# A vision tower on one NeuronCore: the table stage's third power and doublings, one load's queue, and the order of the last group's end

## The chip, the cores and the metric

The kernel runs on one core of one Trainium2 chip. The core has five instruction streams that meet only at semaphores: TensorE (PE in the profile; its weight loads are PEld) for matrix products, VectorE (DVE) and ScalarE (ACT) for elementwise work, GpSimd (POOL), and SyncE (SP), which here only issues transfers. ScalarE issues transfers too. SBUF is the on-chip memory, PSUM the eight banks that TensorE writes. The metric is the device time of one execution, in microseconds (us), lower is better. A profiled execution has a span, from its first to its last instruction, and a time of its own that is a little longer.

## What is computed

The reference builds a state-space convolution kernel from H = 256 channels and N = 64 complex states, and then runs an attention block and a soft decision tree on its result:

```python
dA = (1 + dtA / 2) / (1 - dtA / 2)
V = exp(log(dA)[:, :, None] * arange(256))          # powers 0..255 of one number per (h, n)
h = 2 * einsum('chn,hnl->chl', C * B, V).real       # tokens, (16, 256, 256)
h = h + attention_block(layernorm(h))                # linear attention, gelu MLP
h = h + tree_ffn(layernorm(h))                       # 255 routers, 256 leaves
```

The powers of the number w = dA are products of three short tables: w to the 0..7 (`Er`, `Ei`), B times w to the 0, 8, ..., 56 (`X`, `Y`), and U to the 1..3, where U is w to the 64.

## The kernel before

Each engine's program is written out by hand, and that text is the only thing that sets the order. An engine waits in order: what stands behind a waiting instruction waits with it.

**Table stage.** SyncE loads `log_dt`, both halves of `inv_A_real` (`iar`) and B, ScalarE's queue loads `A_imag` (`aim`). VectorE and ScalarE compute w and square it seven times, in steps of one instruction each (L1009, L1011; ScalarE's squares L627, L630); `base[9]` and `base[10]` hold the squared moduli in turn. On one tile that is 128 partitions (64 states, real and imaginary convention) by 256 channels. Then VectorE forms U's third power (real part in `U[:, 0, 2, :]`, imaginary in `ui[:, 2, :]`) with six operations out of U and its square. Last come three doublings of X and Y: from m entries to 2m, m = 1, 2, 4. The entries of a channel lie together, 8 of X and then 8 of Y, so for m = 1 an operation on X touches one number in every 16. GpSimd meanwhile makes `Er` and `Ei` (L461 to L466).

**Token stage.** Sixteen chunks of 16 channels. For chunk n ScalarE copies the X, Y rows to PSUM (`paired_tables`, L678, which needs the finished X and Y), VectorE makes the products and their sum M (`products`, L1044, `product_sums`, L1052), GpSimd makes the weights Wa and Wb (`rotate`, L494), and TensorE multiplies them (`tokens`, L1480, 64 products). Buffers are double: M of chunk n and the weights of chunk n wait for the tokens of n - 2. ScalarE evicts (`token_out`, L692), and its order for each chunk is: tables of chunk n + 2, token eviction of chunk n, store, Wa's copy and M's copy of chunk n + 2.

**Combined weights.** Before its first token product TensorE multiplies small weight matrices (L1540, L1545) and forms the MLP's bias (L1550, one column each). It begins when the seventh weight, `fc2raw`, has landed. Then `pe_set` is 3; ScalarE copies the bias (L754, `b1copied`), and only after `b1copied` does TensorE go on to chunk 0.

**Middle.** Norms, q, k, v, linear attention, the MLP and the tree run in a software pipeline over groups of four tiles. The change touches none of it.

**The end.** The last group is done in two halves h = 0, 1 of two tiles. For a half: x4 is transposed into one PSUM bank, split into a high and a low part (`last_x4_high` on ScalarE, `last_x4_low` on VectorE), multiplied by the gates (`last_gate`), a tanh, eight levels of the tree on VectorE (`last_tree`), leaf probabilities transposed (`last_lT`) and split (`last_leaf_high`, `last_leaf_low`, L933, L1427), multiplied by the leaves (`last_leaf`), and added to `o1` (`last_finish`, L1434). GpSimd makes `o1` of each half (`last_out_bias`, L597), but only after VectorE's `finish(LAST - 1)` (L1275), which reads the old `o1`. SyncE stores the four tiles (L442).

Of the kernel before, what the change touches and what calls it, by code (L numbers as in the profile page):

```python
# [5 lines left out]
ALU = mybir.AluOpType  # L6
# [4 lines left out]
P = 128  # L11
# [16 lines left out]
LOGS = 8  # L28
# [23 lines left out]
DVE_U = DVE_POWERS + 6 * 4  # L52
# [10 lines left out]
def vit_tower(nc, logdt, inv_ar, a_im, b_ri, c_ri, n1g, n1b, qkvT, projT, proj_b, n2g, n2b, fc1T, fc1_b,  # L63
              fc2T, fc2_b, wq, routersT, leafT, woutT, wout_b, consts, out):
    with ExitStack() as ctx:
# [177 lines left out]
        ld_bias = sem("ld_bias")  # L243
# [37 lines left out]
        def last_out(h):  # L281
            return PS[:, 2 + h, :].rearrange("p (t d) -> p t d", t=2)

# [37 lines left out]
        def _(sp):  # L321
            halves = [slice(r * N, (r + 1) * N) for r in range(2)]
            sp.dma_start(ldt[:, :], logdt.unsqueeze(0).to_broadcast([P, H])).then_inc(ld_exp, 16)
            for rows in halves:
                sp.dma_start(iar[rows, :], inv_ar).then_inc(ld_exp, 16)
# [118 lines left out]
            sp.wait_ge(outst, CREDIT + 32 * LAST + 64)  # L444
# [162 lines left out]
        def _(act):  # L607
            for r in range(2):
                act.dma_start(aim[r * N:(r + 1) * N, :], a_im).then_inc(ld_aim, 16)
# [15 lines left out]
            for j in range(1, LOGS - 1):  # L625
# [4 lines left out]
                act.activation(PS[:, 0, 0:H], power(j)[0], ACT.Square).then_inc(act_tab, 1)  # L630

# [7 lines left out]
            for d in range(ND - 1):  # L639
                if d == 2:  # L640
                    act.wait_ge(dve_set, DVE_POWERS + 6)
                act.activation(U[:, 1, d, :], ui[:, d, :], ACT.Copy, scale=sgn[:, 0:1]).then_inc(u_out, 1)
# [274 lines left out]
            def last_x4_high(h):  # L917
                act.wait_ge(zxT[h], CREDIT + 1)
                act.wait_ge(gtmm, CREDIT + LAST)
                act.activation(last_x(x4Th, h), last_out(h), ACT.Copy).then_inc(zxh[h], 1)  # L920
# [41 lines left out]
            last_leaf_high(1)  # L962


        @block.vector
        def _(dve):
# [47 lines left out]
            t = PS[:, 2, 0:H]  # L1014
            for to, op, first, second in ((U[:, 0, 2, :], ALU.subtract, 0, 1), (ui[:, 2, :], ALU.add, 1, 0)):
                (ar, ai), (br, bi) = power(6), power(7)
                tt(t, ai, (br, bi)[second], ALU.mult)
                tt(to, ar, (br, bi)[first], ALU.mult)
                tt(to, to, t, op)
            dve.wait_ge(b_out, 2)  # L1020
            for j, m in ((0, 1), (1, 2), (2, 4)):
                dve.wait_ge(pw_out, j + 1)
                wr, wi = (PS[:, (6, 7, 1)[j], x * H:(x + 1) * H].unsqueeze(2).to_broadcast([P, H, m])
                          for x in range(2))
                t = PS[:, 2:4, :].rearrange("p b x -> p (b x)")[:, 0:H * m].rearrange("p (h m) -> p h m", m=m)
# [372 lines left out]
            def last_x4_low(h):  # L1398
                dve.wait_ge(zxh[h], CREDIT + 1)
                dve.wait_ge(gtmm, CREDIT + LAST)  # L1400
                dve.tensor_tensor(last_x(x4Tl, h), last_out(h), last_x(x4Th, h).bitcast(F32),
                                  ALU.subtract).then_inc(zxl[h], 1)
# [21 lines left out]
            def last_leaf_low(h):  # L1424
                dve.wait_ge(zlh[h], CREDIT + 1)
                dve.wait_ge(lvmm, CREDIT + LAST)
                dve.tensor_tensor(last_x(lTl, h), last_out(h), last_x(lTh, h).bitcast(F32),  # L1427
                                  ALU.subtract).then_inc(zll[h], 1)
# [31 lines left out]
            last_tree(1, 0, LEVELS)  # L1460
            last_leaf_low(0)
            finish(LAST - 1)
# [6 lines left out]
        def _(pe):  # L1469
# [67 lines left out]
            pe.wait_ge(dve_set, DVE_POWERS)  # L1537
# [342 lines left out]
```

## Time and profile before

| | |
|---|---|
| time, median of 3 runs | 508.58 us (508.49 to 510.35) |
| time of the profiled execution | 508.74 us |
| its span | 507.0 us |
| mean granted TensorE clock | 0.986 |
| busy: PE, DVE, ACT, POOL | 86%, 71%, 57%, 39% of the span |
| TensorE before its first product at 32.06 us | idle |
| chain that ended last, over the whole span | PE 69%, DVE 17%, issue 5%, ACT 4%, POOL 2% |
| landing of fc2raw after its issue | 10.6 us |

The busy shares are means over three unlike stages. In the middle TensorE never stops; in the first 73 us and in the last 15 us it waits, and there the chain of waits names other engines. A time in the views is counted from the start of the span.

### The profile page before, as it was taken

To read this page: it belongs to the slowest core of one execution; us is meant where nothing else is said; L and a number is where in the kernel's file an instruction comes from. 1 tells how busy PE (TensorE), PEld (TensorE's weight loads), DVE (VectorE), ACT (ScalarE), POOL (GpSimd) and SP (SyncE) were. 2 spreads that over 40 slices of the span, in tenths; PEclk is the share of its full clock that TensorE was granted. 3 is DMA by queue.
4 is the path that set the end of the run, shared out by engine and by line. 5 is a ranking of instruction groups with operands and counts; after the bars stand their busy time and mean duration, and the time that the engine had idled before them with its cause. 6 is when DMAs were issued, how large, how long until landed. Compare 5 with 4: busy or idle time off the path is not lost.

```text
span 507.0 us, 11410 instructions
## 1 busy us (share of the span) xinstructions
PE 434.1 (86%) x3808; PEld 398.1 (79%) x3808; DVE 357.8 (71%) x870; ACT 291.1 (57%) x604; POOL 195.5 (39%) x185
## 2 busy tenths in 40 slices
PE   0047663999899999999999999999999999998974
PEld 0037653888788898888988988988988988998973
DVE  5899998995877685547476476476476576485684
ACT  3805553788876777566457457457447448446630
POOL 0497998761241210515406306306307207206001
PEclk9998997999999999999999999999999999999998
DMA  4532665344343101101002002002002001001002
GB/s 125 184 127 75 166 170 172 95 137 138 112 121 100 63 22 43 41 1 43 1 1 83 0 0 83 0 0 83 0 0 83 0 0 41 0 0 43 3 0 84
DMA packets 39903, 30.95 MB, mean 61 GB/s; under 512 B 19520, under 2 KB 35264, under 8 KB 39872
## 3 DMA queue, kind: packets, MB, share of 16 engines
q1 hardware_dynamic: 29312, 27.81, 17.9%
q10 hardware_dynamic: 10560, 2.75, 2.3%
q8 instruction: 16, 0.26, 0.2%
q14 instruction: 15, 0.12, 0.1%
HBM read 17.97 MB, written 12.58 MB: 60 GB/s over the span
## 4 chain that ended last, share of the span: by engine, by line
PE 69%; DVE 17%; issue 5%; ACT 4%; POOL 2%; DMA 1%; DVEq 1%; SPq 0%; POOLq 0%; ACTq 0%
PE PS L315 18%; PE PS L317 18%; PE PS L316 18%; PE PS L1488 5%; PE PS L1598 3%; PE PS L1530 3%; PE PS L1480 3%; DVE M L1052 2%; DVE Mb L1044 2%; DVE XY L976 2%; DVE lTl L1215 1%; DVE PS L976 1%; PE PS L1497 1%; DVE outb L1275 1%; DVE PS L1044 1%
## 5 line engine op out<-in xcount | busy, mean ns | idle before, releaser
L1244 DVE TENSOR_TENSOR gl<-PS,gh 128x512 fp32r<-128x512 f32 x56 | 38.7, 690 | 62.2 <-ACT gh L811 34.4
L808 ACT ACTIVATE PS<-PS,fc1bias 128x512 f32<-128x512 f32 x56 | 36.7, 656 | 75.2 <-PE PS L317 74.3
L315 PE MATMUL PS<-fc2h,gh 128*128 128x256 f32 x256 | 73.7, 288 | 2.9 <-DVE gl L1244 1.5
L542 POOL TENSOR_SCALAR pst<-mv 128x4 f32<-128x4 f32 x15 | 4.2, 282 | 185.3 <-DVE pst L1228 185.3
L317 PE MATMUL PS<-fc2l,gh 128*128 128x256 f32 x256 | 71.5, 279 | 0.0
L316 PE MATMUL PS<-fc2h,gl 128*128 128x256 f32 x256 | 71.4, 279 | 0.0
L315 PE MATMUL PS<-x2Th,fc1h 128*128 (+2 forms) x144 | 54.4, 378 | 0.0
L315 PEld LDWEIGHTS PS<-fc2h,gh 128*128 128x128 f32 x256 | 48.0, 188 | 7.0 <-DVE pst L1228 1.6
L316 PE MATMUL PS<-x2Th,fc1l 128*128 (+2 forms) x144 | 53.0, 368 | 0.0
L317 PE MATMUL PS<-x2Tl,fc1h 128*128 (+2 forms) x144 | 52.9, 367 | 0.0
L1480 PE MATMUL PS<-M,Wa 128*64 128x64 f32 x512 | 35.1, 237 | 16.7 <-DVE M L1052 14.8
L316 PEld LDWEIGHTS PS<-fc2h,gl 128*128 128x128 f32 x256 | 48.2, 188 | 1.0
L317 PEld LDWEIGHTS PS<-fc2l,gh 128*128 128x128 f32 x256 | 48.0, 188 | 0.0
L1480 PEld LDWEIGHTS PS<-M,Wa 128*64 128x64 f32 x512 | 32.2, 146 | 19.6 <-DVE M L1052 12.8
L811 ACT ACTIVATE gh<-PS 128x512 fp32r<-128x512 f32 x56 | 33.6, 599 | 2.8
L1480 PE MATMUL PS<-M,Wb 128*64 128x64 f32 x512 | 34.3, 233 | 0.0
L1480 PEld LDWEIGHTS PS<-M,Wb 128*64 128x64 f32 x512 | 32.2, 149 | 0.0
L1540 PE MATMUL PS<-routraw,wqraw 128*128 128x256 f32 x8 | 3.8, 654 | 32.1 <-DMA fc2raw<-in_fc2T 32.1
L317 PEld LDWEIGHTS PS<-x2Tl,fc1h 128*128 128x128 f32 x144 | 27.1, 188 | 4.7
L494 POOL TENSOR_TENSOR Wa<-craw,U 128x768 f32<-128x768 f32 x16 | 25.7, 1607 | 9.9 <-PE PS L1480 7.7
L315 PEld LDWEIGHTS PS<-x2Th,fc1h 128*128 128x128 f32 x144 | 27.1, 189 | 2.5
L316 PEld LDWEIGHTS PS<-x2Th,fc1l 128*128 128x128 f32 x144 | 27.2, 189 | 2.3
(233 smaller groups left out, 1402.7 us busy)
## 6 DMA issues: line engine op xcount, KB each, us to landing
h<-h_scratch SPq DMA_DIRECT2D x16, 256.0 KB, 3.7
q_scratch<-qe SPq DMA_DIRECT2D x16, 256.0 KB, 2.2
qf<-q_scratch SPq DMA_DIRECT2D x16, 256.0 KB, 2.9
out_tokens<-outb SPq DMA_DIRECT2D x14, 256.0 KB, 2.3
h_scratch<-tokev ACTq DMA_DIRECT2D x10, 256.0 KB, 3.0
craw<-in_c_ri SPq DMA_DIRECT2D x16, 128.0 KB, 2.6
craw<-in_c_ri SPq DMA_DIRECT2D x32, 64.0 KB, 2.4
h_scratch<-tokev SPq DMA_DIRECT2D x6, 256.0 KB, 2.8
```

Source lines behind the costliest of these rows:

```text
L315: pe.matmul(dst, ah, bh, start=start, stop=False, **kw)
L316: pe.matmul(dst, al, bh, start=False, stop=False, **kw)
L317: return pe.matmul(dst, ah, bl, start=False, stop=stop, **kw)
L494: pool.tensor_tensor(w[:, par, :, :, 1:ND].rearrange("p h c d -> p d h c"), c, u, ALU.mult).then_inc(wdone, 1)
L808: act.activation(bank(j % 2), bank(j % 2), ACT.Gelu, bias=fc1bias[:, j:j + 1]).then_inc(gact, 1)
L811: act.activation(gh[:, j % 2, :], bank(j % 2), ACT.Copy).then_inc(gact, 1)
L976: link(dve.tensor_tensor(out_, a, b, op))
L1044: dve.tensor_tensor(to, x, w, ALU.mult).then_inc(vdone, 1)
L1244: dve.tensor_tensor(gl[:, j % 2, :], bank(j % 2), gh[:, j % 2, :].bitcast(F32), ALU.subtract).then_inc(gldone, 1)
L1480: mm = pe.matmul(dst, w[:, par, i, :, :].rearrange("p c d -> p (c d)"), M[:, par, i, :, :].rearrange("p a e -> p (a e)"), start=x == 0, st ...
L1488: mm = pe.transpose(PS[:, b + k, t * P:(t + 1) * P], src[:, t, k * P:(k + 1) * P], ident)
L1530: mm = pe.matmul(PS[:, sums_bank(c), k * (P + 1):(k + 1) * (P + 1)], key, value, start=half == 0 and k == 0, stop=half == 1, skip_group_ch ...
```

## The change

- **Third power.** With s = 4 times the square of U's real part, the third power's imaginary part is (s - modulus squared) times U's imaginary part, and its real part is (s - 3 times modulus squared) times U's real part. The square of the real part was already in PSUM, and ScalarE makes the threefold modulus with one more operation.
- **Doublings.** X and Y are multiplied by the real part in one operation over both. For m = 1 and 2 the sum is one operation as well.
- **Load.** The second half of `iar` is issued first on ScalarE's queue instead of third on SyncE's.
- **End.** For half 1 each transposed column block has a PSUM bank of its own (`last_turned`), and the copies, low parts and products go block by block; `last_rows_out` now runs over the block outside and the tile inside, for both halves. VectorE takes `last_leaf_low(0)` after level 4 of the second tree instead of after its last level. The odd tiles are stored from ScalarE's queue.
- TensorE's wait for the tables before its weight products names a count two higher.

```diff
             sp.dma_start(ldt[:, :], ...).then_inc(ld_exp, 16)
-            for rows in halves:
-                sp.dma_start(iar[rows, :], inv_ar).then_inc(ld_exp, 16)
+            sp.dma_start(iar[halves[0], :], inv_ar).then_inc(ld_exp, 16)
...
             for half in range(HALVES):
-                for c in range(2):
-                    sp.wait_ge(zout[half], CREDIT + c + 1)
-                    sp.dma_start(out[2 * LAST + c, half * P:(half + 1) * P, :],
-                                 x2[:, 2 * half + c, :]).then_inc(outst, 16)
+                sp.wait_ge(zout[half], CREDIT + 1)
+                sp.dma_start(out[2 * LAST, ...], x2[:, 2 * half, :]).then_inc(outst, 16)
...
         def _(act):
+            act.dma_start(iar[N:P, :], inv_ar).then_inc(ld_exp, 16)
             for r in range(2):
                 act.dma_start(aim[r * N:(r + 1) * N, :], a_im).then_inc(ld_aim, 16)
...
+            act.wait_ge(act_tab, 5 + 2 * (LOGS - 2))
+            act.activation(base[:, 9, :], base[:, 10, :], ACT.Copy, scale=3.0).then_inc(act_tab, 1)
...
             def last_leaf_high(h):
-                act.wait_ge(zlT[h], CREDIT + 1)
                 act.wait_ge(lvmm, CREDIT + LAST)
-                act.activation(last_x(lTh, h), last_out(h), ACT.Copy).then_inc(zlh[h], 1)
+                if h == 0:
+                    act.wait_ge(zlT[h], CREDIT + 1)
+                    act.activation(last_x(lTh, h), last_out(h), ACT.Copy).then_inc(zlh[h], 1)
+                else:
+                    for k in range(KD):
+                        act.wait_ge(zlT[h], CREDIT + k + 1)
+                        act.activation(lTh[:, k, HT:2 * HT], last_turned(h, k), ACT.Copy).then_inc(zlh[h], 1)
+            def last_store(half):
+                act.wait_ge(zout[half], CREDIT + 2)
+                act.dma_start(out[2 * LAST + 1, ...], x2[:, 2 * half + 1, :]).then_inc(lastst, 16)
...
-            for to, op, first, second in ((U[:, 0, 2, :], ALU.subtract, 0, 1), (ui[:, 2, :], ALU.add, 1, 0)):
-                (ar, ai), (br, bi) = power(6), power(7)
-                tt(t, ai, (br, bi)[second], ALU.mult)
-                tt(to, ar, (br, bi)[first], ALU.mult)
-                tt(to, to, t, op)
+            link(dve.scalar_tensor_tensor(PS[:, 3, 0:H], ur2, 4.0, base[:, 10, :], ALU.mult, ALU.subtract))
+            dve.wait_ge(act_tab, 7 + 2 * (LOGS - 2))
+            link(dve.scalar_tensor_tensor(PS[:, 2, 0:H], ur2, 4.0, base[:, 9, :], ALU.mult, ALU.subtract))
+            tt(ui[:, 2, :], PS[:, 3, 0:H], ui1, ALU.mult)
+            tt(U[:, 0, 2, :], PS[:, 2, 0:H], ur, ALU.mult)
...
-                tt(t, y, wi, ALU.mult)
-                tt(x_, x, wr, ALU.mult)
-                tt(x_, x_, t, ALU.add)
-                tt(t, x, wi, ALU.mult)
-                tt(y_, y, wr, ALU.mult)
-                tt(y_, y_, t, ALU.subtract)
+                if m < 4:
+                    tt(t, xy, wr, ALU.mult)
+                    tt(x_, y, wi, ALU.mult)
+                    link(dve.scalar_tensor_tensor(y_, x, -1.0, wi, ALU.mult, ALU.mult))
+                    tt(xy_, xy_, t, ALU.add)
+                else:
+                    tt(xy_, xy, wr, ALU.mult)
+                    tt(t, y, wi, ALU.mult)
+                    tt(x_, x_, t, ALU.add)
+                    tt(t, x, wi, ALU.mult)
+                    tt(y_, y_, t, ALU.subtract)
...
-            last_tree(1, 0, LEVELS)
+            last_tree(1, 0, 5)
             last_leaf_low(0)
+            last_tree(1, 5, LEVELS)
             finish(LAST - 1)
             last_leaf_low(1)
...
-            pe.wait_ge(dve_set, DVE_POWERS)
+            pe.wait_ge(dve_set, DVE_POWERS + 2)
...
-                for t in range(2):
-                    x = slice(h * HT + t * P, h * HT + (t + 1) * P)
-                    for k in range(KD):
+                for k in range(KD):
+                    if h == 1 or k == 0:
+                        pe.wait_ge(high, CREDIT + k + 1)
+                        pe.wait_ge(low, CREDIT + k + 1)
+                    for t in range(2):
+                        x = slice(h * HT + t * P, h * HT + (t + 1) * P)
                         mm = three(pe, last_rows(h, t), ah[:, k, x], al[:, k, x], wh[:, k, :], wl[:, k, :],
                                    k == 0, k == KD - 1)
-                    mm.then_inc(done, 1)
+                        if k == KD - 1:
+                            mm.then_inc(done, 1)
```

Below is VectorE's program in the table stage before, from the first operation of the third power through the first half of the m = 1 doubling (its last two rows come once more for Y). PS is PSUM, XY holds X and Y, U and ui the powers of U.

```order
L976 TENSOR_TENSOR PS<-ui 128x256
L976 TENSOR_TENSOR U<-U 128x256
L976 TENSOR_TENSOR U<-U,PS 128x256
L976 TENSOR_TENSOR PS<-ui,U 128x256
L976 TENSOR_TENSOR ui<-U,ui 128x256
L976 TENSOR_TENSOR ui<-ui,PS 128x256
L976 TENSOR_TENSOR PS<-XY,PS 128x256
L976 TENSOR_TENSOR XY<-XY,PS 128x256 x2
```

And the same place in the changed kernel, through the whole m = 1 doubling:

```order
L1035 SCALAR_TENSOR_TENSOR PS<-PS,base 128x256
L1037 SCALAR_TENSOR_TENSOR PS<-PS,base 128x256
L996 TENSOR_TENSOR ui<-PS,ui 128x256
L996 TENSOR_TENSOR U<-PS,U 128x256
L996 TENSOR_TENSOR PS<-XY,PS 128x512
L996 TENSOR_TENSOR XY<-XY,PS 128x256
L1053 SCALAR_TENSOR_TENSOR XY<-XY,PS 128x256
L996 TENSOR_TENSOR XY<-XY,PS 128x512
```

Six operations have become four, each with an operand in PSUM, and the six of a doubling have become four, two of them twice as wide.

The second place is VectorE's end, before: th, lpA and lpB are the tree's tiles, lTl the low part of the leaf probabilities, outb the tile of the group before the last, x the last group's result.

```order
L1418 SCALAR_TENSOR_TENSOR lpA<-th,lpB 128x2x16
L1421 SCALAR_TENSOR_TENSOR lpA<-lpB,lpA 128x2x16
L1418 SCALAR_TENSOR_TENSOR lpB<-th,lpA 128x2x32
L1421 SCALAR_TENSOR_TENSOR lpB<-lpA,lpB 128x2x32
L1418 SCALAR_TENSOR_TENSOR lpA<-th,lpB 128x128
L1421 SCALAR_TENSOR_TENSOR lpA<-lpB,lpA 128x128
L1418 SCALAR_TENSOR_TENSOR lpB<-th,lpA 128x256
L1421 SCALAR_TENSOR_TENSOR lpB<-lpA,lpB 128x256
L1427 TENSOR_TENSOR lTl<-PS,lTh 128x2x256
L1275 TENSOR_TENSOR outb<-PS,o_132 128x512 x2
L1427 TENSOR_TENSOR lTl<-PS,lTh 128x2x256
L1434 TENSOR_TENSOR x_123<-PS,o_132 128x256 x4
```

And in the changed kernel:

```order
L1456 SCALAR_TENSOR_TENSOR lpA<-lpB,lpA 128x2x16
L1463 TENSOR_TENSOR lTl<-PS,lTh 128x2x256
L1453 SCALAR_TENSOR_TENSOR lpB<-th,lpA 128x2x32
L1456 SCALAR_TENSOR_TENSOR lpB<-lpA,lpB 128x2x32
L1453 SCALAR_TENSOR_TENSOR lpA<-th,lpB 128x128
L1456 SCALAR_TENSOR_TENSOR lpA<-lpB,lpA 128x128
L1453 SCALAR_TENSOR_TENSOR lpB<-th,lpA 128x256
L1456 SCALAR_TENSOR_TENSOR lpB<-lpA,lpB 128x256
L1304 TENSOR_TENSOR outb<-PS,o_132 128x512 x2
L1468 TENSOR_TENSOR lTl<-PS,lTh 128x256 x2
L1475 TENSOR_TENSOR x_123<-PS,o_132 128x256 x4
```

The low part of half 0 has moved ahead of the last six tree operations; that of half 1 is two narrow operations, still behind `finish`.

## Rows read from the trace of the kernel before

**Rows 1.** Chain of waits, 0 to 80 us: start, us, what.
```profile
1.80 3.41 DMA iar<-in_inv_ar
...
19.20 0.45 DVE PS L976
...
23.10 0.62 DVE PS L976
...
38.86 0.40 ACT PS L678
...
73.17 2.15 PE PS L1480 x64
```
**Rows 2.** Timeline, SyncE's queue at the start: start, us, engine, line, operation.
```profile
1.19 1.19 SPq L325 DMA_DIRECT2D iar<-in_inv_ar  x2
```
**Rows 3.** Groups by form, 19 to 39 us: count, busy us, mean ns, idle before.
```profile
L976 DVE TENSOR_TENSOR XY<-XY,PS 128x1024 f32<-128x1024 f32 x4 | 4.9, 1220 | 0.1
...
L976 DVE TENSOR_TENSOR XY<-XY,PS 128x512 f32<-128x512 f32 x4 | 2.8, 688 | 0.1
L976 DVE TENSOR_TENSOR XY<-XY,PS 128x256 f32<-128x256 f32 x4 | 2.5, 614 | 0.1
...
L976 DVE TENSOR_TENSOR ui<-U,ui 128x256 f32<-128x256 f32 x1 | 1.2, 1153 | 0.0
...
L1011 DVE SCALAR_TENSOR_TENSOR U<-PS,base 128x256 f32<-128x256 f32 x1 | 0.4, 425 | 0.1
```
**Rows 4.** Timelines by engine, 32 to 50 us, in order of time.
```profile
32.06 3.78 PE L1540 MATMUL PS<-routraw,wqraw 128*128 128x256 f32 x8 [32.06 <-DMA fc2raw<-in_fc2T]
...
37.46 3.63 PE L1550 MATMUL PS<-nrm,fc1raw 128*128 128x1 f32 x32
...
41.13 0.18 ACT L754 ACTIVATE b1add<-PS 128x8 f32<-128x8 f32 x1
...
42.78 0.49 PE L1480 MATMUL PS<-M,Wa 128*64 128x64 f32 x4 [1.69 <-DVE M L1052]
...
46.40 0.60 ACT L692 ACTIVATE tokev<-PS 128x512 f32<-128x512 f32 x1 [3.84 <-PE PS L1480]
...
46.74 1.64 POOL L494 TENSOR_TENSOR Wa<-craw,U 128x768 f32<-128x768 f32 x1 [2.92 <-PE PS L1480]
...
48.54 0.47 ACT L678 ACTIVATE PS<-XY 128x256 f32 x1
...
49.62 1.10 DVE L1044 TENSOR_TENSOR PS<-PS,Er 128x896 f32<-128x896 f32 x1 [0.15 <-DVE M L1052]
```
**Rows 5.** Windows: stretch, busy of each engine, then granted clock, DMA share, GB/s.
```profile
44.00:45.00 1.00, 1.00 (x24) 1.00 (x23) 0.97 (x1) 0.00 (x0) 0.00 (x0) 0.50 0.28 77
...
496.00:498.00 2.00, 1.51 (x7) 1.54 (x8) 1.54 (x3) 0.00 (x0) 0.32 (x1) 0.66 0.00 0
```
**Rows 6.** Timelines by engine, 493 to 504 us, in order of time.
```profile
493.68 0.23 DVE L1418 SCALAR_TENSOR_TENSOR lpB<-th,lpA 128x64 f32<-128x64 f32 x1
...
495.66 0.68 DVE L1427 TENSOR_TENSOR lTl<-PS,lTh 128x512 fp32r<-128x512 f32 x1
...
496.26 1.28 DVE L1275 TENSOR_TENSOR outb<-PS,o 128x512 f32<-128x512 f32 x2
...
496.49 0.43 PE L315 MATMUL PS<-leafh,lTh 128*128 128x256 f32 x1 [3.96 <-DVE lTl L1427]
...
500.16 0.60 ACT L933 ACTIVATE lTh<-PS 128x512 fp32r<-128x512 f32 x1 [7.00 <-PE PS L1757]
...
503.27 0.42 DVE L1434 TENSOR_TENSOR x<-PS,o 128x256 f32<-128x256 f32 x1 [0.18 <-PE PS L317]
```
**Rows 7.** Source lines L597 and L442: duration ns min/median/max, first and last start.
```profile
L597 POOL TENSOR_TENSOR o<-h,woutbias x2: 1273/1273/1273, 497.7 to 498.9; 128x512 f32<-128x512 f32 x2
...
L442 SPq DMA_DIRECT2D out_tokens<-x x4: 345/432/1627, 501.8 to 504.8; - x4
DMA to landing us min/median/max: 1.8/2.5/3.6
```

More of the change, by code:

```diff
@@ L282, in last_out, with last_turned @@
             return PS[:, 2 + h, :].rearrange("p (t d) -> p t d", t=2)
+        def last_turned(h, k):
+            return PS[:, 2, k * HT:(k + 1) * HT] if h == 0 else PS[:, (3, 2)[k], 0:HT]
         def last_rows(h, t):
@@ L962, in _ @@
             last_leaf_high(1)
+            last_store(0)
+            last_store(1)
         @block.vector
@@ L1398, in last_x4_low @@
             def last_x4_low(h):
-                dve.wait_ge(zxh[h], CREDIT + 1)
                 dve.wait_ge(gtmm, CREDIT + LAST)
-                dve.tensor_tensor(last_x(x4Tl, h), last_out(h), last_x(x4Th, h).bitcast(F32),
-                                  ALU.subtract).then_inc(zxl[h], 1)
+                if h == 0:
+                    dve.wait_ge(zxh[h], CREDIT + 1)
+                    dve.tensor_tensor(last_x(x4Tl, h), last_out(h), last_x(x4Th, h).bitcast(F32),
+                                      ALU.subtract).then_inc(zxl[h], 1)
+                else:
+                    for k in range(KD):
+                        dve.wait_ge(zxh[h], CREDIT + k + 1)
+                        dve.tensor_tensor(x4Tl[:, k, HT:2 * HT], last_turned(h, k), x4Th[:, k, HT:2 * HT].bitcast(F32),
+                                          ALU.subtract).then_inc(zxl[h], 1)
             def last_tree(h, first, last):
@@ L1424, in last_leaf_low @@
             def last_leaf_low(h):
-                dve.wait_ge(zlh[h], CREDIT + 1)
                 dve.wait_ge(lvmm, CREDIT + LAST)
-                dve.tensor_tensor(last_x(lTl, h), last_out(h), last_x(lTh, h).bitcast(F32),
-                                  ALU.subtract).then_inc(zll[h], 1)
+                if h == 0:
+                    dve.wait_ge(zlh[h], CREDIT + 1)
+                    dve.tensor_tensor(last_x(lTl, h), last_out(h), last_x(lTh, h).bitcast(F32),
+                                      ALU.subtract).then_inc(zll[h], 1)
+                else:
+                    for k in range(KD):
+                        dve.wait_ge(zlh[h], CREDIT + k + 1)
+                        dve.tensor_tensor(lTl[:, k, HT:2 * HT], last_turned(h, k), lTh[:, k, HT:2 * HT].bitcast(F32),
+                                          ALU.subtract).then_inc(zll[h], 1)
             def last_finish(h):
@@ L1756, in last_transposes, with last_rows_out @@
                     for t in range(2):
-                        mm = pe.transpose(PS[:, 2 + h, k * HT + t * P:k * HT + (t + 1) * P],
+                        mm = pe.transpose(last_turned(h, k)[:, t * P:(t + 1) * P],
                                           src[:, 2 * h + t, k * P:(k + 1) * P], ident)
-                mm.then_inc(done, 1)
-            def last_rows_out(h, ah, al, wh, wl, done):
-                for t in range(2):
-                    x = slice(h * HT + t * P, h * HT + (t + 1) * P)
-                    for k in range(KD):
+                    if h == 1 or k == KD - 1:
+                        mm.then_inc(done, 1)
+            def last_rows_out(h, high, low, ah, al, wh, wl, done):
+                for k in range(KD):
+                    if h == 1 or k == 0:
[3 more added lines that the diff above has]
+                        x = slice(h * HT + t * P, h * HT + (t + 1) * P)
                         mm = three(pe, last_rows(h, t), ah[:, k, x], al[:, k, x], wh[:, k, :], wl[:, k, :],
                                    k == 0, k == KD - 1)
-                    mm.then_inc(done, 1)
+                        if k == KD - 1:
+                            mm.then_inc(done, 1)
             def last_x4(h):
```

39 lines of the change are left out of this document (23 added, 16 removed).

## The prediction, made before the changed kernel was run

> **What bounds the kernel now.** I read the chain of waits first, since the busy shares are means over three stages. From 6 to 73 us the chain names VectorE almost without a break, and SyncE's loads before it [rows 1]. From about 95 to 491 us it is nearly all TensorE, and nothing in the change touches that stretch: it moves as a whole. The last 15 us are a relay in which each engine waits for one other [rows 6]. So the change is worth what it takes off the two ends, if no other wait takes over. The sum has two terms, one for each end.
>
> **The load.** The chain begins with the second half of `iar`: its issue starts at 1.80 us and it is there 3.41 us later [rows 1]. Two issues take 1.19 us on SyncE's queue [rows 2], so 0.6 each. With one of them on ScalarE's queue, issued at once, the last of the three loads starts at 1.2 and lands at 4.6: 0.6 us earlier. `aim` now stands behind `iar` on ScalarE's queue, 0.6 later: its second half issues at 1.9 and lands near 5.3. It is asked for only after two exponentials and one VectorE operation of some 0.4 each, at 5.8, so it is covered, by half a microsecond. Everything behind on SyncE's queue is 0.6 earlier too, the seven weights among it.
>
> **The third power.** Its six operations run from 19.20 to 23.10 [rows 1], 3.90 us, because one with both inputs in SBUF took 1153 ns beside GpSimd's work where an operation with an input in PSUM took 425 [rows 3]. The four new ones each have a PSUM input: 4 x (0.425 + 0.035 between two) = 1.84. Gain 2.06. ScalarE's extra operation (0.4) falls between its last square and the copies that wait for the last power; the second new operation needs it some 0.9 us after that square begins, and it is ready then. If it isn't, the cost is below 0.3.
>
> **The doublings.** From the forms [rows 3]: 1220 ns for 1024 numbers and 688 for 512 give 1.04 ns a number and 0.155 fixed. For m = 1, where each number lies 16 from the next, 256 numbers take 614: 1.79 ns each.
> - m = 1: before 6 x 0.65 = 3.9. After, two of 256 (1.3) and two of 512, whose numbers lie 8 apart. At 1.04 a number such a wide one is 0.72 with its gap, at 1.79 it is 1.11. No row has a stride of 8 on VectorE. I take 1.11, since the row with single scattered numbers is nearer than the one with neighbours: after 3.5, gain 0.4 (1.15 at the other end).
> - m = 2: 6 x 0.725 = 4.35 against 2 x 0.725 + 2 x 1.255 = 3.96: gain 0.4.
> - m = 4: 6 x 1.255 = 7.53 against 4 x 1.255 + 2.32 (2048 numbers) = 7.34: gain 0.2.
>
> The Trainium skill ("SBUF — State Buffer", "Door 1: The DMA port swizzle") has SBUF in 16-byte lines, so that strides up to four fp32 numbers are free and wider ones pay for each line. That speaks against the widened m = 1 operations, for a stride of 8 is still beyond a line; by it they cost the 1.11 and not the 0.72. It would leave m = 2 alone, where two neighbours share a line, and the trace agrees there (688 for 512).
>
> VectorE thus gains 2.06 + 0.4 + 0.4 + 0.2 = 3.0 us (3.8 at most), with the load 3.6 (4.4): X and Y are whole at 35.3 and no longer at 38.86 [rows 1].
>
> **What is late next.** TensorE. Its weight products begin when fc2raw lands, at 32.06, and end at 37.46 + 3.63 = 41.1 [rows 4]. Only then comes ScalarE's L754, at 41.13, and only behind that chunk 0. Before, this was hidden: chunk 0 waited for M until 42.78, 1.7 us idle [rows 4]. Now M would be there at 39.2, but TensorE ends its weight products at 40.5 (0.6 earlier with the loads) and starts chunk 0 at 40.75. Chunk 0 took 3.62 us before (42.78 to the eviction at 46.40 [rows 4]), at a granted clock of 0.50, the 1.2 GHz level [rows 5]; a chunk at full clock takes 2.15 [rows 1]. Behind the eviction ScalarE stores, copies Wa and M and makes chunk 3's table 2.14 us later, at 48.54, and VectorE's products of chunk 3, at 49.62, need that table [rows 4]: eviction + 2.65 at the earliest. Before, that left 0.55 us of slack.
>
> Which clock will chunk 0 have? It fell to 1.2 GHz just before chunk 0, after the L1550 products of one column each and 1.7 us idle; now the idle time is 0.25 us, but the single columns are still there and give the array little to do. I take most of it at half clock: 3.3 us. Eviction at 44.1, products of chunk 3 at 46.75 against 49.62 before: **first term 2.85 us**, not VectorE's 3.6. Bounds: all at half clock and the weights landing no earlier, 2.0; all at full clock, eviction at 42.95 and products at 45.6, which lets VectorE's 3.6 through and caps its best case at 4.0. From chunk 4 on VectorE's three operations of 1.1 a chunk stay the longest, above GpSimd's two, which overlap; GpSimd starts chunk 2 0.35 us behind the eviction as before [rows 4] and catches up.
>
> **The end.** Before: the low part of half 0 waits for the whole second tree and runs at 495.66, TensorE's product of half 0 starts at 496.49, at a mean clock of 0.66 over those 2 us, and only behind it come half 1's transposes, ScalarE's copy at 500.16, the low part, the product, and the last addition until 503.27 + 0.42 = 503.7 [rows 5, 6]. After: the low part of half 0 goes in at 493.7, where level 5 stood [rows 6]; TensorE does half 0 from 494.5 to 496, beside the tree. The tree's rest ends 0.7 later, near 496.4, and `finish` where it did, near 497.6 (I add 0.1 for x4's low part, now two operations). Half 1's transposes start at 496.5, its copies and low parts follow block by block, VectorE's behind `finish` until 498.5, and the product ends near 499.9.
>
> What is late next here is GpSimd: o1 is begun when `finish` is done, 497.7, the second half at 498.9 and 1.27 long [rows 7], so 500.2, with my 0.1 at 500.3. The last two additions (0.75 together) end at 501.1: 2.6 us earlier, where TensorE alone would have given 3.
>
> **The stores.** The last addition ended at 503.7, but the fourth store was issued at 504.8, because the third issue took 1.63 us, and it landed 1.8 later [rows 7]; 0.4 us after that the span ended. Two queues with two stores each start the last one at once. With the median landing of 2.5 the span ends at 501.15 + 2.5 + 0.4 = 504.05: **second term 3.0 us**. With the slow issue again 2.6, with a landing of 1.8 3.65, with half 1's product at half clock (12 products of 0.21 instead of 0.12, past GpSimd's end) some 2.3.
>
> **The sum.** 2.85 + 3.0 = 5.85. The profiled execution took 508.74, so 502.9; it is 0.16 above the median of the runs, 508.58, which gives **502.7 us**. What moves runs apart goes both ways.
>
> **Rivals.**
> 1. *The clock stays up behind the weight products.* For it: TensorE is idle for only 0.25 us. Against: before the fall, too, it was busy with single columns. The first term is then 3.6 to 4.0, the time 508.6 - 6.8 = 501.8. The Trainium skill ("TensorE: Matmul & The Clock Gate", "What's actually happening") lets recent activity decide the level, and its observation point runs free of the kernel, so the same program can show either; by it this rival and my forecast could both occur in one series.
> 2. *The ends give back less.* Weights that land no earlier and a full chunk at half clock (2.0), half 1's product at half clock or the slow store issue again (2.4): 4.4, so 504.2. For it: the clock at 496 to 498 was at half level for two thirds of the stretch [rows 5]; against it: that was behind an idle TensorE, which now works at 494.5.
> 3. *Slower: the wide operations are slow.* An operation whose real factor is repeated over X and Y, through four dimensions, has no row. 2 x 512 + 2 x 1024 + 2048 = 5120 numbers go through such operations. VectorE has 0.75 us of slack against the eviction, so it takes 0.75 + 5.85 = 6.6 us more, 1.3 ns a number above 1.04, to undo both terms: from 2.3 ns a number the change is slower. At 3.1 it costs 10.5 - 6.6 = 3.9, and the time is 512.5. Nothing in the rows is beyond 1.79.
>
> That the change doesn't do what it says is a small case: if `aim` is late, 0.6 falls to 0.1 or so.
>
> **Chances.** Forecast 0.5, rival 1 0.26, rival 2 0.21, rival 3 0.02, the rest lower gains. The range reaches from 501.0 (both best bounds nearly together) to 504.9 (2.0 + 1.7). Within 0.5% (2.5 us) is no difference to this measurement; that needs more than half of both terms to fail: 0.05. Faster 0.93, slower 0.02.
>
> **What would show it.** The first exponential at 4.6; the third power 1.85 long; the m = 1 wide operations near 1.07 and the 2048 one near 2.3; ScalarE's L754 waiting for TensorE at 40.5, where before it waited for nothing; VectorE idle before chunk 3's product, with a release by ScalarE's table; a granted clock of 0.50 in chunk 0. At the end VectorE waiting for GpSimd's o1 before its last additions, and a last store issued within 0.1 of the last addition. The forecast is wrong if VectorE never waits for the table (rival 1), if the last additions wait for TensorE, or if the middle changes its length.

## The result, and the profile after

The changed kernel took 505.27 us (median of five runs, 504.49 to 506.72); the kernel before, on the same chip, 509.39 (508.49 to 510.35). The ratio is 0.9929, with a 95% interval of 0.9907 to 0.9951. That is 3.6 us less (2.5 to 4.7), where 5.85 were forecast; the medians lie 4.1 apart. The time is outside the range of 501.0 to 504.9. The profiled execution of the changed kernel took 506.72 us, with a span of 504.9.

The table work on VectorE, in groups by form, 18 to 37 us (count, then busy us and mean ns, then idle before):

```profile
L996 DVE TENSOR_TENSOR XY<-XY,PS 128x2048 f32<-128x2048 f32 x1 | 2.3, 2289 | 0.0
...
L996 DVE TENSOR_TENSOR PS<-XY,PS 128x512 f32<-128x512 f32 x1 | 1.1, 1119 | 0.0
...
L1035 DVE SCALAR_TENSOR_TENSOR PS<-PS,base 128x256 f32<-128x256 f32 x1 | 0.4, 432 | 0.0
```

Set against [rows 3]: the third power now takes four operations of 0.43, from 18.88 to 20.69 us, and the wide operations cost what was forecast: 1119 ns for 512 numbers that lie 8 apart, 2289 for 2048.

What came of it, in timelines by engine, 30 to 49 us, to be read against [rows 4]:

```profile
30.71 3.78 PE L1582 MATMUL PS<-routraw,wqraw 128*128 128x256 f32 x8 [30.71 <-DMA fc2raw<-in_fc2T]
34.29 3.10 PE L1587 MATMUL PS<-woutraw,leafraw 128*128 128x256 f32 x8
37.22 4.16 PE L1592 MATMUL PS<-nrm,fc1raw 128*128 128x1 f32 x32
42.24 0.49 PE L1522 MATMUL PS<-M,Wa 128*64 128x64 f32 x4 [0.87 <-DVE Mb L1073]
...
41.41 0.18 ACT L758 ACTIVATE b1add<-PS 128x8 f32<-128x8 f32 x1 [3.50 <-PE PS L1592]
46.01 0.60 ACT L696 ACTIVATE tokev<-PS 128x512 f32<-128x512 f32 x1 [3.16 <-PE PS L1522]
...
36.26 1.10 DVE L1073 TENSOR_TENSOR PS<-PS,Er 128x896 f32<-128x896 f32 x1 [0.68 <-ACT PS L682]
...
48.90 1.10 DVE L1073 TENSOR_TENSOR PS<-PS,Er 128x896 f32<-128x896 f32 x1 [1.71 <-ACT PS L682]
```

X and Y were whole at 35.6 us and not at 38.86. The weights landed 1.35 us earlier than before: fc2raw was issued 0.63 earlier, at 20.82, and took 9.8 us to land instead of 10.6, which varies by itself (9.5 in low_early, an experiment below that has the loads of before). But the weight products ended at 41.38, no earlier than before, because they took 10.66 us in place of 9.0; chunk 0 started at 42.24, and VectorE then lost 1.71 us waiting for chunk 3's table. Chunk 3's products are 0.7 us earlier than before, where VectorE alone had won 3.25.

The windows (busy of PE, PEld, DVE, ACT, POOL, then granted clock, DMA share, GB/s) show the level in chunk 0 and at the end:

```profile
38.00:40.00 2.00, 2.00 (x20) 2.00 (x19) 1.81 (x3) 0.00 (x0) 1.86 (x2) 1.00 0.55 152
40.00:42.00 2.00, 1.38 (x8) 1.29 (x7) 1.97 (x3) 0.58 (x3) 1.89 (x2) 0.53 0.28 72
42.00:44.00 2.00, 1.75 (x32) 1.76 (x33) 1.74 (x2) 0.85 (x3) 1.04 (x1) 0.50 0.01 4
...
496.00:498.00 2.00, 2.00 (x11) 2.00 (x11) 1.91 (x4) 0.00 (x0) 0.00 (x0) 0.50 0.00 0
...
500.00:502.00 2.00, 2.00 (x11) 2.00 (x10) 0.48 (x2) 0.00 (x0) 0.60 (x1) 0.50 0.58 201
```

And the end, in timelines by engine, against [rows 6]:

```profile
494.09 0.69 DVE L1463 TENSOR_TENSOR lTl<-PS,lTh 128x512 fp32r<-128x512 f32 x1
496.66 1.28 DVE L1304 TENSOR_TENSOR outb<-PS,o 128x512 f32<-128x512 f32 x2
...
498.34 0.75 ACT L947 ACTIVATE lTh<-PS 128x256 fp32r<-128x256 f32 x2 [4.59 <-PE PS L1799]
...
501.77 0.99 DVE L1475 TENSOR_TENSOR x<-PS,o 128x256 f32<-128x256 f32 x2 [1.52 <-PE PS L320]
```

The order is the forecast one: the low part stands ahead of the tree's end, ScalarE's copy comes 1.8 us earlier, the last addition ends at 502.76 and not at 503.7. But the last wait is for TensorE, which worked at 1.2 GHz from 494 to 502 us, and not for GpSimd. By the prediction's own list that is a sign of being wrong.

Four marks locate the time in one profiled execution of each kernel: VectorE's first normalisation of a token group (`xh`), the first low part at 481 to 485 us (`lTl`), the end of the last addition, and the end of the span. Between `xh` and `lTl` the code of all thirteen is the same but for five_warm_mid. The kernels other than before and changed are the experiments, explained in the next section.

| kernel | xh | lTl | xh to lTl | lTl to last addition | to the span's end | median, us | ratio to before (95%) |
|---|---|---|---|---|---|---|---|
| before | 81.81 | 483.38 | 401.6 | 20.3 | 3.3 | 509.39 | 1 |
| changed | 81.40 | 484.05 | 402.7 | 18.7 | 2.1 | 505.27 | 0.9929 (0.9907 to 0.9951) |
| table_only | 80.45 | 482.75 | 402.3 | 20.5 | 2.7 | 507.91 | 0.9990 (0.9973 to 1.0007) |
| end_only | 81.32 | 482.94 | 401.6 | 17.3 | 2.2 | 505.37 | 0.9939 (0.9917 to 0.9962) |
| low_early | 81.98 | 484.25 | 402.3 | 18.1 | 2.1 | 506.42 | 0.9945 (0.9929 to 0.9961) |
| stores_only | 81.90 | 483.54 | 401.6 | 20.3 | 2.7 | 508.49 | 0.9990 (0.9975 to 1.0004) |
| five_weights | 78.53 | 481.12 | 402.6 | 17.5 | 3.1 | 502.04 | 0.9864 (0.9844 to 0.9885) |
| warm_front | 78.50 | 481.02 | 402.5 | 17.5 | 2.2 | 502.64 | 0.9885 (0.9864 to 0.9907) |
| singles_first | 81.19 | 483.91 | 402.7 | 17.5 | 2.2 | 505.64 | 0.9938 (0.9915 to 0.9960) |
| before_five | 81.68 | 484.43 | 402.8 | 21.7 | 2.2 | 509.16 | 1.0010 (0.9996 to 1.0025) |
| warm_end | 81.67 | 484.20 | 402.5 | 17.4 | 2.2 | 503.83 | 0.9887 (0.9865 to 0.9909) |
| five_warm | 78.44 | 480.80 | 402.4 | 17.4 | 2.3 | 502.22 | 0.9860 (0.9839 to 0.9882) |
| five_warm_mid | 78.47 | 485.43 | 407.0 | 17.3 | 2.2 | 505.53 | 0.9946 (0.9921 to 0.9971) |

The ratios are each to the runs of the kernel before on the same chip, whose medians were 508.3 to 509.6. An interval reaches some 1.1 us to either side, and the difference of two such ratios some 1.6. The fourth column says how far single executions can be trusted: the same code took 401.6 to 402.8 us. The profiled execution of the kernel before drew the short end and that of the changed kernel a long one, which hides 1.1 us in a comparison of these two traces alone. The clock goes along with it: in before, end_only and stores_only (401.6) the first transposes behind `xh`, at 82 to 83 us, ran at full clock (0.66 us for four), and in the nine with 402.3 or more at half (1.11 to 1.12). Whether that is the cause wasn't tested.

### The profile page after: what moved, and what is told of

Same layout as the page of the kernel before. It is cut to its first block, busy times and chain, and to the rows that moved or that the text cites. A ratio compares the mean times of both kernels' runs of the same rounds, so it can differ in the third digit from the quotient of the medians.

```text
span 504.9 us, 11412 instructions
## 1 busy us (share of the span) xinstructions
PE 438.8 (87%) x3808; PEld 402.2 (80%) x3808; DVE 355.0 (70%) x865; ACT 291.6 (58%) x607; POOL 194.9 (39%) x185
## 4 chain that ended last, share of the span: by engine, by line
PE 68%; DVE 14%; issue 6%; POOL 4%; ACT 4%; DMA 2%; DVEq 0%; POOLq 0%; SPq 0%; ACTq 0%
PE PS L318 18%; PE PS L320 17%; PE PS L319 17%; PE PS L1530 5%; PE PS L1522 3%; PE PS L1640 3%; PE PS L1572 3%; POOL Wb L495 2%; DVE XY L996 2%; DVE lTl L1244 1%; PE PS L1539 1%; DVE PS L996 1%; DVE outb L1304 1%; POOL Wa L495 1%; DMA h<-h_scratch 1%
```

## The experiments

**Which half of the change is worth what.** table_only is the kernel before with the four operations for U's third power, the wide doublings and TensorE's higher count. end_only is the kernel before with the new end: half 1 block by block, `last_leaf_low(0)` after level 4, the odd tiles stored by ScalarE. No run has the changed load alone.

> The kernel before with the third power, the doublings and TensorE's count alone; the load and the end stay. Theory A (the weight products and the bias copy stand in front of chunk 0, so that the 2.9 us that VectorE gains are lost in a wait for chunk 3's table): X and Y whole 2.9 us earlier than before, at 36.0, but chunk 3's products at 48.5 to 49.2 and no longer 49.62, and the time 0.5 to 1.2 us below before. Rival B (the table stage carries the gain): 2.5 to 3 us below before.

> The kernel before with the end of the change alone: banks by block, low part of half 0 after level 4, products block by block, stores on two queues. Theory A (the two ends add, and the end gives 2.5 to 3 us whatever the front does, of which about 1.1 is the last store no longer standing behind a slow issue): 2.5 to 3 us below the kernel before, and TensorE's product of half 0 at half clock (0.21 a product), so that half 1's transposes wait for it and not for the tree. Rival B (the end gives nothing of its own, the 4 us come from the table stage): within 1 us of before.

Measured, by the ratios: 0.5 us less for the tables (from 1.4 less to 0.4 more) and 3.1 less for the end (1.9 to 4.2). So the tables alone are not told apart from no change, their rival B of 2.5 to 3 us is excluded, and the end has a gain of its own. table_only, timelines:

```profile
32.20 3.71 PE L1551 MATMUL PS<-routraw,wqraw 128*128 128x256 f32 x8 [32.20 <-DMA fc2raw<-in_fc2T]
...
41.15 0.18 ACT L756 ACTIVATE b1add<-PS 128x8 f32<-128x8 f32 x1 [3.00 <-PE PS L1561]
...
48.29 1.10 DVE L1055 TENSOR_TENSOR PS<-PS,Er 128x896 f32<-128x896 f32 x1 [1.70 <-ACT PS L680]
```

`b1add` comes when it came before, at 41.15, but it now waits 3.0 us for TensorE, and VectorE waits 1.70 for the table. VectorE's first products came 3.0 us earlier than before (36.50 and not 39.51); of that, 1.7 went into the wait, and 1.3 was left at chunk 3 in this execution (48.29 against 49.62). end_only, the chain that ended last:

```profile
495.54 1.29 DVE outb L1293 x2
...
496.97 1.28 POOL o L599
498.25 1.25 POOLq L65
499.52 0.42 DVE x L1464
```

With the clock up at the end (1.00 from 490 to 502; the expectation had it at half) the chain runs as predicted: `finish`, GpSimd's o1 of 2.5 us, the last additions.

**Which part of the end.** low_early moves half 0's low part ahead of the second tree's last levels, and nothing else; stores_only only moves the odd tile of each half to ScalarE's queue. Both start from the kernel before.

```diff
- last_tree(1, 0, LEVELS)      # low_early: the one edit
+ last_tree(1, 0, 5)
  last_leaf_low(0)
+ last_tree(1, 5, LEVELS)
```

> The kernel before with one other part of the change alone: half 0's low part of the last level is transposed and its products run ahead of the tree's last level. Theory A (the product of half 0 leaves the path from the tree's end to the last additions; its three passes and the low part stand beside the tree): 1.5 to 2 us below the kernel before. Rival B (GpSimd's o of 2.5 us or TensorE at half clock sets the end anyway): less than 0.7 us. Rival C (VectorE's low part of half 0 now delays the tree itself by its 0.7 us): 0 to 1 us gained.

> The kernel before with one part of the change alone: half 1's stores go out on ScalarE's and SyncE's queues. Theory A (the stores are worth what lies between the last addition and the span's end: 3.3 us before, 2.1 in the changed kernel): about 1.1 us below the kernel before, ratio near 0.998. Rival B (the slow store issue of 1.63 us was an accident of one execution): no difference, the last addition to the span's end stays near 3.3 us in both or near 2.1 in both.

low_early measured 2.8 us less (2.0 to 3.6), not told apart from the whole end's 3.1; the interval just touches its theory A of 1.5 to 2. In its profile 2.2 us (of end_only's 3.0) stand between `lTl` and the last addition, and 1.2 behind it, in stores that it doesn't change. Its TensorE:

```profile
495.27 0.55 PE L315 MATMUL PS<-leafh,lTh 128*128 128x256 f32 x1 [1.86 <-DVE lTl L1427]
...
497.97 0.77 PE L1758 MATMUL PS<-const,lpB 128*128 128x128 f32 x4
```

Half 0's twelve products stand beside the tree, 2.7 us at 1.2 GHz, and half 1's transposes start at 497.97 where before they started at 499.07. stores_only was not told apart from no change (0.9990, the interval includes 1). The slow issue did not belong to the queue, either: low_early has all four stores on SyncE's queue, as before, and against [rows 7] they read

```profile
L442 SPq DMA_DIRECT2D out_tokens<-x x4: 332/339/432, 500.5 to 502.4; - x4
...
DMA to landing us min/median/max: 1.7/1.7/1.8
```

From the last addition to the span's end one queue took 2.1 to 3.3 us and two queues 2.1 to 3.1 (table). So none of this term is shown as the edit's: stores_only's ratio gives 0.5 us, with an interval from 1.3 less to 0.2 more.

**Is TensorE's wait for the weights what eats the tables' gain?** The five weights that the products read get a semaphore of their own, and projraw and fc2raw are issued after them as before; before_five is the same edit in the kernel before.

```diff
- pe.wait_ge(ld_w2, 16 * 7)
+ pe.wait_ge(ld_w5, 16 * 5)
```

> The changed kernel with a semaphore of its own for the first five weights, so that TensorE begins its weight products when fc1raw has landed (near 26) and not when fc2raw has (30.7). Theory A: the products and the bias copy are over by 37, chunk 0 starts when its M is there (39.5), at half clock, is evicted by 43.3, chunk 3's products start at 46.1 to 46.4 in place of 48.90: 2.5 us below the changed kernel, some 6.3 below before. Rival B (VectorE's gain is lost later, at GpSimd's weights of 3 us a chunk or the load of h0): chunk 3 earlier, but the first norm's operation (81.4) less than 1 us earlier, and the time like the changed kernel's.

> The kernel before, with TensorE's weight products waiting only for the five weights' own transfers: the control for five_weights. Theory A (before the change the table X and Y, whole at 38.9 us, and VectorE bound the front; TensorE's wait for the last weight bound nothing): the weight products end near 36.5, chunk 0 starts with its M near 42.8 as before, and the time is the kernel before's within 0.5 us. Rival B (the earlier products are worth their 3 us by themselves, whatever the table does): 2 to 3 us below the kernel before.

five_weights came out at 502.04 us, 0.9864: some 3.3 us below the changed kernel by the ratios. Its timelines:

```profile
27.67 3.63 PE L1585 MATMUL PS<-routraw,wqraw 128*128 128x256 f32 x8 [27.67 <-POOL Er L466]
...
39.53 0.49 PE L1525 MATMUL PS<-M,Wa 128*64 128x64 f32 x4 [3.03 <-DVE M L1084]
...
46.37 1.10 DVE L1076 TENSOR_TENSOR PS<-PS,Er 128x896 f32<-128x896 f32 x1 [0.15 <-DVE M L1084]
```

TensorE waits 3.03 us for M, VectorE's products of chunk 3 start at 46.37 without waiting for the table, and `xh` comes at 78.53 in place of 81.40: 2.9 of the 3.3 us stand there. Theory A holds. In the kernel before, the same edit gives nothing (1.0010): there chunk 0 started at 42.67, with TensorE idle 6.1 us before it. So the wait cost nothing until the tables were faster: the table edit and the wait together are worth 3 us and more, each alone 0.5 or nothing, and neither of these two is told apart from zero.

**Is it the wait, or how long the products take behind it?** 14 products of the constants (28 passes in the records) run ahead of the wait, their results read by nothing; the wait itself stays. singles_first instead puts the single-column products first; ScalarE's `b1add` still waits for all three groups.

```diff
+ pe.wait_ge(ld_const, 16 * 6)
+ pe.wait_ge(dve_set, DVE_POWERS + 6)
+ for _ in range(14):
+     pe.matmul(PS[:, 5, 0:D], ident, const[:, 0:D], start=True, stop=True)
  pe.wait_ge(ld_w2, 16 * 7)
  pe.wait_ge(pool_set, 1)
- pe.wait_ge(ld_const, 16 * 6)
- pe.wait_ge(dve_set, DVE_POWERS + 2)
```

> The changed kernel with 14 products of the constants more, whose results nothing reads, on TensorE from about 22.5 us on, ahead of its wait for the weights. Theory A (chunk 0 came late because TensorE was cold: the weight products took 10.66 us, 31 us to 41.4, and chunk 0 3.74): the 256-column weight products take 391 ns each instead of 654, all of them about 7 to 8 us, so they end at 38 to 39 us, chunk 0's eviction ends before 44, chunk 3's products start near 46.5 as with the five weights' own semaphore, and the time is 1.5 to 2.5 us below the changed kernel. Rival B (the clock falls again during the single-column products whatever came before): the products end near 40.5, chunk 0 at half clock, and the time is 0 to 1 us below the changed kernel. Rival C (the 14 products last beyond 30.7 us and hold the weight products up): the changed kernel's time or up to 1 us more.

> The changed kernel with TensorE's bias products of one column each put ahead of the two weight products. Theory C (it is the clock in chunk 0 that costs: single columns let it fall, full products hold it): chunk 0 starts at the same time, about 41.5 to 42.2, but takes 2.15 us in place of 3.74, its eviction is 1.5 us earlier, and the time 1.3 to 1.6 us below the changed kernel. Rival D (the clock falls by chance whatever comes ahead): chunk 0 at half clock as before, and the time like the changed kernel's.

warm_front took 502.64 us, 0.9885, 2.2 us below the changed kernel by the ratios. Its TensorE:

```profile
22.59 8.64 PE L1579 MATMUL PS<-const 128*128 128x256 f32 x28 [22.59 <-DVE XY L996]
31.06 1.89 PE L1584 MATMUL PS<-routraw,wqraw 128*128 128x256 f32 x8
32.78 1.89 PE L1589 MATMUL PS<-woutraw,leafraw 128*128 128x256 f32 x8
34.51 4.01 PE L1594 MATMUL PS<-nrm,fc1raw 128*128 128x1 f32 x32
39.51 0.49 PE L1522 MATMUL PS<-M,Wa 128*64 128x64 f32 x4 [0.99 <-DVE M L1081]
```

The same eight passes (four products in the kernel; the profile counts two passes for each, and 32 for the 16 single-column products) take 1.89 us behind a busy TensorE and 3.78 behind an idle one. The weight products end at 38.5, 2.9 us before those of the changed kernel, chunk 0 waits for M, and VectorE's products of chunk 3 start at 46.35 with no wait. Theory A holds. The clock did fall again within the single columns, as rival B had it (0.90 in 36 to 38 us), and chunk 0 ran at 0.50 (38 to 44 us): the clock in chunk 0, which the prediction weighed at such length, did not matter once it started early enough. singles_first shows the same from the other side:

```profile
31.12 6.99 PE L1582 MATMUL PS<-nrm,fc1raw 128*128 128x1 f32 x32 [31.12 <-DMA fc2raw<-in_fc2T]
37.97 3.36 PE L1587 MATMUL PS<-routraw,wqraw 128*128 128x256 f32 x8
...
43.96 0.34 PE L1522 MATMUL PS<-M,Wa 128*64 128x64 f32 x4 [0.91 <-ACT b1add L758]
```

Behind an idle TensorE the single columns take 6.99 us and not 3.63. Chunk 0 then ran at full clock, as its theory C had it, in 2.17 us up to its eviction, but it started at 43.96 and not at 42.24, and the eviction still began only at 46.13: the time is not told apart from the changed kernel's.

**The clock at the end.** 18 products more between half 0's transposed low part and its product; five_warm has them and the five weights' semaphore.

```diff
+ pe.wait_ge(zth[1], CREDIT + 2)
+ for _ in range(18):
+     pe.matmul(last_rows(1, 0), x4Th[:, 0, 0:P], gateh[:, 0, :], start=True, stop=True)
```

> The changed kernel with 18 products more, whose results nothing reads, on TensorE between half 0's transposed low part and half 0's last product, so that TensorE is busy before the end. Theory A (the end of the changed kernel is set by TensorE at half clock: 2.9 us a half): the granted clock is 1.00 in the last 8 us, half 1's transposes wait for the tree and not for TensorE, the last addition waits for GpSimd's o, and the time is 0.7 to 1.4 us below the changed kernel. Rival B (the clock at the end is at full anyway in most executions, and only the one profiled was slow): no difference or 0.5 us more, since the dummy products stand in the path.

> The changed kernel with both: TensorE's weight products wait only for the five weights' own transfers, and the 18 products more ahead of the end. Theory A (the two losses are independent, one in the front and one at the end): five_weights' 502.0 less 0.7 to 1.4, so 500.7 to 501.4 us. Rival B (the time that the front gains is lost again in the clock's low stretches, or the dummy products cost as much as they give): 502 us or more.

warm_end took 503.83 us, 0.9887. In its profile the clock is 1.00 in every window from 494 to 502, and the last addition waits for GpSimd:

```profile
499.56 0.76 DVE L1475 TENSOR_TENSOR x<-PS,o 128x256 f32<-128x256 f32 x2 [0.80 <-POOL o L598]
500.80 0.76 DVE L1475 TENSOR_TENSOR x<-PS,o 128x256 f32<-128x256 f32 x2 [0.48 <-POOL o L598]
```

`lTl` to the last addition is 17.4 us and not 18.7: theory A, 1.3 us. By the medians it gained 1.4, by the ratios 2.1 with an interval of some 1.6 to either side. But five_warm (502.22) gained nothing over five_weights (502.04), against its theory A. The table says why: five_weights already had 17.5. There the clock was low for half 0's product alone (0.50 at 492 to 494) and up for half 1's, and one half at 1.2 GHz costs 0.1 to 0.2 us, since its product runs beside other work. warm_front and singles_first, low for half 0 alone, have 17.5 too. Only where both halves ran low, as in the profiled execution of the changed kernel, did the end lose 1.3 us; with the old end it is the same, 21.7 in before_five against 20.3 in before. How often that happens isn't settled by one profile a kernel.

**The clock in the middle.** five_warm_mid adds 56 products to five_warm around the first transposes of y, since the clock was half from about 78 to 88 us.

```diff
  if s == -1:                                   # before and after y_transposes(0)
+     for _ in range(28):
+         pe.matmul(PS[:, 5, 0:D], qkvh[:, 0, 0:P], qkvh[:, 0, 0:D], start=True, stop=True)
```

> The kernel with the five weights' own semaphore and the warm end, and 56 products more, whose results nothing reads, around the first transposes of y (chunk 11, from about 70 us on), where TensorE's clock was half until 91 us. Theory A (the half clock from 81 to 91 us makes tokens of chunk 11 take 3.7 instead of 2.15 us and takes back a part of the front's gain): TensorE full from 80 us on, 1 to 2 us below five_warm, so 500.2 to 501.2 us. Rival B (VectorE or the load of h bounds that stretch, so that the clock there is free): 502 us. Rival C (the dummy products stand in the way of the first transposes): 503 us or more.

Measured: 505.53 us, 3.3 above five_warm by the medians and 4.4 by the ratios. That median stands in a gap: six of the twelve runs took 503.6 to 504.3 us and six 506.7 to 508.7, and the profiled one (506.75) is of the upper group. So what follows is told of that group. The clock was up (1.00 from 66 to 100 us) and chunk 11 took 2.15 us, but the number is rival C's, for another reason than the one it named. five_warm_mid:

```profile
83.61 0.34 PE L1525 MATMUL PS<-M,Wa 128*64 128x64 f32 x4 [0.34 <-DVE M L1084]
...
85.84 1.95 DVE L1115 TENSOR_SCALAR xh<-h,mv,pst 128x256 f32<-128x256 f32 x2
87.70 1.45 DVE L1119 SCALAR_TENSOR_TENSOR mr<-mv,pst 128x2 f32<-128x2 f32 x1
...
86.07 1.57 POOL L497 TENSOR_TENSOR Wa<-craw,U 128x768 f32<-128x768 f32 x1
87.54 1.70 POOL L497 TENSOR_TENSOR Wb<-craw,U 128x768 f32<-128x768 f32 x1
...
94.97 1.62 POOL L497 TENSOR_TENSOR Wa<-craw,U 128x768 f32<-128x768 f32 x1 [4.04 <-PE PS L1525]
96.44 1.75 POOL L497 TENSOR_TENSOR Wb<-craw,U 128x768 f32<-128x768 f32 x1
...
95.28 3.11 DVE L1144 SCALAR_TENSOR_TENSOR kvm<-ke,kr 128x256 f32<-128x256 f32 x2
```

and five_warm at the same place:

```profile
85.81 0.71 DVE L1115 TENSOR_SCALAR xh<-h,mv,pst 128x256 f32<-128x256 f32 x2
86.43 0.15 DVE L1119 SCALAR_TENSOR_TENSOR mr<-mv,pst 128x2 f32<-128x2 f32 x1
...
87.50 1.61 POOL L497 TENSOR_TENSOR Wa<-craw,U 128x768 f32<-128x768 f32 x1 [1.27 <-PE PS L1525]
...
93.15 0.73 DVE L1144 SCALAR_TENSOR_TENSOR kvm<-ke,kr 128x256 f32<-128x256 f32 x2
```

The products stood in nobody's way: chunk 11 starts at 83.6 in both. It ended earlier, so GpSimd began its two wide operations at 86.07 and not at 87.50, into VectorE's normalisation, whose first two steps then took 1.95 and 1.45 us in place of 0.71 and 0.15. The Trainium skill ("SBUF — State Buffer", "Who interferes with whom") has a pair of ports that the two engines take in turn, each for a whole instruction; the trace agrees, since `mr`, an operation on two numbers, ends within 0.1 us (89.15) of GpSimd's second operation (89.24). That makes the start of the next VectorE products 2.6 us later (89.15 against 86.57). VectorE, late, then runs into the next pair of wide operations: `kvm` took 3.11 us at 95.28 where five_warm's took 0.73 before that pair began, and again 3.05 at 104.43. The next two starts of VectorE's products are 4.5 and 6.75 us later than in five_warm (98.31 and 107.40 against 93.79 and 100.65), and 4.6 of that is left at `lTl`. Why half the runs were spared a part of it isn't shown.

## Why the prediction was wrong

- **The load.** In the two profiled executions 0.33 us measured (first exponential at 4.91 and not 5.24), 0.6 predicted. The last of the three loads was issued at 1.20, as forecast, but took 3.68 us to land where it had taken 3.41 [rows 1].
- **Third power and doublings.** Right: 1.85 us for the third power against 1.84, 1.10 and 1.12 for the wide m = 1 operations against 1.07 to 1.11, 2.29 against 2.3. X and Y were whole at 35.6, predicted 35.3. That wide operations 8 numbers apart pay the scattered price was borne out (1119 ns), so rival 3 had nothing behind it.
- **What is late next: TensorE.** The mechanism was right in each link, `b1add` behind the weight products, chunk 0, its eviction, chunk 3's table. The first term, what is left of the tables' gain at chunk 3, is the step that failed, in its size. The prediction said "TensorE ends its weight products at 40.5 (0.6 earlier with the loads) and starts chunk 0 at 40.75", eviction at 44.1. They ended at 41.38, chunk 0 started at 42.24, the eviction began at 46.01. Of the 1.9 us, 0.9 lie in the end of the weight products: they began 0.75 earlier than forecast and took 1.6 longer, since their time was taken over from [rows 4] as if it were fixed. 0.6 lie in the way over `b1add` into chunk 0, on which TensorE stood idle 0.87 to 0.91 us in the changed kernel, table_only and singles_first where I allowed 0.25; before, it was hidden behind M. 0.4 lie in chunk 0, 3.77 us long and not 3.35, all of it at 1.2 GHz. Another 0.2 come between the eviction and the products. **The first term** was 0.7 us at chunk 3 in the profiled execution and 0.5 by table_only's ratio (without the load), not 2.85: below the lower bound of 2.0, which had the products at the same length and 0.25 us for the way into the loop. warm_front shortens the products and five_weights takes the wait away; they give back 2.2 and 3.3 us by the ratios.
- **What the clock was argued from.** The prediction weighed the short idle time, which spoke for rival 1, against the single columns, which spoke for half clock. In the changed kernel the level fell at 40.1 us (1.00 in 38 to 40, 0.53 in 40 to 42), while TensorE still ran the single columns, before any idle time, and with them first (singles_first) chunk 0 ran at 1.00. So half clock in chunk 0 was forecast right and on the right ground.
- **Rival 1** (the clock stays up behind the weight products) did not occur in the changed kernel. In table_only it did for a part of chunk 0 (its eviction 3.4 us behind the start), with the weights landing later, and chunk 3 came 1.3 us earlier than before and not 3.6 to 4.0. It named the clock of chunk 0, while the time of the weight products counted more.
- **The end.** **The second term** was 3.0 us predicted; end_only measured 3.1, and the marks of the changed kernel give 1.6 + 1.2 = 2.8 between `lTl` and the span's end, and those of end_only 3.0 + 1.1. "What is late next here is GpSimd" held in end_only and warm_end and not in the profiled execution of the changed kernel, where TensorE was low for both halves; rival 2 had that case, at 2.3. The stores' part of it was luck: the slow third issue in [rows 7] was of that execution, not of the queue, and the two queues show no gain of their own; what made the sum come out is that the last additions came 3.0 us earlier behind `lTl` in end_only, where 2.6 were forecast.
- **The middle.** Forecast to move as a whole. It grew by 1.1 us between the two profiled executions, which the prediction names as a sign of being wrong; but executions of the same code differ by that much (table), along with the clock at its start.
- **The sum.** 0.5 + 3.1 = 3.6, as measured, in place of 2.85 + 3.0. Each of the three has an interval of about 1 us to either side, so that they agree to 0.1 is luck.

The range failed with its lower bound for the first term: it held two unknowns (when the weights land, which clock chunk 0 has) and took two durations beside them for certain.

## What to carry to other kernels

When a faster engine uncovers a wait, forecast the uncovered chain with its own links: the row that stood beside other work shows neither the way into the loop behind it nor how long the same products take from another start. Work taken off the bound is worth little until what is late next moves too; here one wait, for a transfer that the products behind it don't read, was worth about as much as the whole end (3.3 and 3.1 us). A kernel that beats both is five_weights, 502.04 us; and before an engine is made faster, look at which engine it then runs into.

## What was not expected of the hardware

- The same eight passes of 256 columns took 3.78 us behind an idle TensorE and 1.89 behind a busy one, and 32 single-column ones 6.99 or 3.63, while the granted clock read 1.00 from 30 to 34 us in the changed kernel and in warm_front alike. Behind an idle stretch the durations tell, and the column doesn't. Why the second eight took 3.10 us in the changed kernel and 2.99 in warm_end, but 1.89 in table_only, low_early and end_only, behind nearly the same idle time, stays open.
- Beside GpSimd's 768-wide operations VectorE's tensor_scalar from SBUF, 0.35 us alone, took 1.2 us more, an operation on two numbers 1.3 more, and two of 256 numbers 3.11 us where they take 0.73.
- A store's issue took 0.34 us in most rows, 0.89 in one of five_weights and 1.63 in one of before, with landings of 1.7 to 3.6; SyncE's queue alone showed both ends of that, in before (up to 1.63 and 3.6) and low_early (at most 0.43 and 1.8).
